# One step in thirteen of a graph attention gather, fetched row by row from SyncE and ScalarE

## The chip, the cores and the metric

The kernel runs on one core of a Trainium2 chip. The metric is the device time of one execution in microseconds (us), lower is better. Times below are medians of several executions; the profile is of one execution, recorded by the hardware profiler.

## The reference

One graph attention layer with a residual, over 12,500 nodes of 128 features and 412,500 edges of 64 features. The edges are sorted by target, and there are 4 heads of 32:

```python
h = maximum(layernorm(x), 0)
h = (h @ W_node.T).reshape(nodes, 4, 32)
e = (edge_attr @ W_edge.T).reshape(edges, 4, 32)
att = sum(concat([h[src], h[tgt], e], -1) * a, -1)
att = where(att > 0, att, 0.2 * att)
m = maximum(segment_max(att, tgt), 0)
ex = exp(att - m[tgt])
denom = segment_sum(ex, tgt) + (num_edges - deg)[:, None] * exp(-m)
out = x + segment_sum((ex / denom[tgt])[:, :, None] * h[src], tgt)
```

## The kernel before, in words

**Layout.** The sorted edges are padded and cut into 128 runs of T = 3224 edges, one run to a partition. One step is one edge of every partition, and a block is KB = 13 steps, so that there are 248 blocks. A node's row, 136 floats (544 bytes), lies in DRAM in `rows`: for each head 32 features and a one, then the four source logits.

**Setup.** The first stretch counts edges per node, projects the nodes, writes `rows` to DRAM, and builds the target logits `td`, which stay in SBUF for all edges.

**The block loop.** Eight blocks (UN) are unrolled; the first eight run outside the loop and the loop repeats them 30 times. For block i each engine has its own program, and engines meet in semaphores alone:

- GpSimd (`body`, L327) waits until the multiply of block i - 4 has read its slot group (`val_done`), then issues 13 indirect gathers (L334, by the helper at L291). Each fetches 128 rows, one to a partition, by one column of `idx`. There are SLOTS = 4 slot groups, so gathers may run up to four blocks ahead.
- VectorE first forms the logits of block i (`logits`, from L540; it waits for the gathers at L544), with small operations on 52 or 56 columns, and then the sums of block i - 1 (`sums`, from L568): a multiply of rows with weights (L571, signals `val_done`), a carry copy, and one scan (L581, signals `scanned`).
- ScalarE (`body`, L394) makes two exponentials (L399, L401) for block i, and copies the state of block i - 1 out of the scan's tile into `R` (`copy_state`, L412), which frees that tile and hands `R` to SyncE.
- SyncE (`body`, L261) stores `R` to DRAM (`store`, L257), loads the edge features of two blocks at once (L270), and every fourth block the node numbers of the next four (L266).
- TensorE multiplies the edge features with the edge weights, two blocks at once (L732).

Every engine takes its own instructions in the order in which they are written, and the DMAs that SyncE and GpSimd issue stand in those same orders. The addresses of DMAs in the loop hang on the loop's counter, so each is preceded by small register instructions on the issuing engine.

**Tail.** GpSimd fetches the last state of each node from DRAM, VectorE divides and adds x, and SyncE stores the output.

Of the kernel before, what the change touches and what calls it, by code (L numbers as in the profile page):

```python
# [4 lines left out]
P = 128  # L5
# [7 lines left out]
NP = P * W  # L13
T = 3224
KB = 13
BLOCKS = T // KB
PAIRS2 = BLOCKS // 2
SLOTS = 4
# [4 lines left out]
CL = 512  # L23
# [5 lines left out]
STEPS = W // NG  # L29
UN = 8  # L30
ITERS = BLOCKS // UN
RING = 8
PIECES = 8
PT = T // PIECES


def graph_attention_kernel(nc, x, x_t, src, dstf, dst16, lasts, ends, first, ea, w_node, w_node_t, a_blk, we2,
                           ident_c, centre_c, cols_c, out):
    fp32, bf16, i32, i16 = mybir.dt.float32, mybir.dt.bfloat16, mybir.dt.int32, mybir.dt.int16
    ALU = mybir.AluOpType  # L40
# [1 line left out]
    ds = bass.ds  # L42
# [8 lines left out]
    with ctx:  # L51
        def sb(name, shape, dt):
            return ctx.enter_context(nc.sbuf_tensor(name, shape, dt))
# [4 lines left out]
        def sem(name):  # L58
            return ctx.enter_context(nc.semaphore(name))
# [3 lines left out]
        hT = big[:, 0:NP]  # L63
        xr = big[:, 0:NP].rearrange("p (w d) -> p w d", d=D)
        idx = sb("idx", [P, 2, SLOTS * KB], i32)
        slots = sb("slots", [P, SLOTS * KB, ROW], fp32)
        V = sb("V", [P, 2, ROW * COL], fp32)
        R = sb("R", [P, 2, KB, ROW], fp32)
# [85 lines left out]
        idx_dma = [sem(f"idx_dma{k}") for k in range(2)]  # L154
        ea_dma = [sem(f"ea_dma{k}") for k in range(2)]
        gather_dma = [sem(f"gather_dma{k}") for k in range(SLOTS)]
        store_dma = [sem(f"store_dma{k}") for k in range(2)]
        ae_done, logits_done, d_ready, w_ready, a_ready, val_done, scanned, copied = (
            sem("ae_done"), sem("logits_done"), sem("d_ready"), sem("w_ready"), sem("a_ready"), sem("val_done"),
# [2 lines left out]
            sem("end_packed"), sem("end_t"), sem("mf_done"), sem("fac_done"), sem("sf_done"), sem("end_back"),  # L162
            sem("fix_gather"), sem("fix_max"), sem("fix_exp"), sem("fix_ready"), sem("fix_dma"))
        get_dma = [sem(f"get_dma{k}") for k in range(STEPS)]
        slots_taken = sem("slots_taken")
        em_done, group_done, stored = sem("em_done"), sem("group_done"), sem("stored")
        x_again = [sem(f"x_again{k}") for k in range(STEPS // 2)]

# [2 lines left out]
        def after(eng, s, v):  # L171
            if not (isinstance(v, int) and v <= 0):
                eng.wait_ge(s, v)  # L173

        def loop(eng, body):
            for q in range(UN):
# [44 lines left out]
        @block.sync  # L221
        def _(sp):
            sp.dma_start(last_b[:, :], lasts.broadcast_to([P, CL])).then_inc(loaded_lasts, 16)
            sp.dma_start(cols[:, :], cols_c).then_inc(loaded_lasts, 16)
            for a, b in ((w_raw, w_node), (we_raw, we2), (a_sb, a_blk), (centre, centre_c), (ident, ident_c)):
                sp.dma_start(a[:, :], b).then_inc(loaded_w, 16)
            sp.dma_start(w_ext[:, 0:D], w_node_t).then_inc(loaded_w, 16)
            for g in range(STEPS):
                sp.dma_start(hT[:, g * NG * P:(g + 1) * NG * P], x_t[:, g * NG * P:(g + 1) * NG * P]).then_inc(loaded_x[g], 16)
            sp.dma_start(dst_s, dstf).then_inc(loaded_dst, 16)  # L230
            sp.dma_start(ends_s[:, :], ends).then_inc(loaded_ends, 16)
            sp.dma_start(first_i[:, :], first).then_inc(loaded_ends, 16)
            sp.wait_ge(zeroed, 1)
            sp.dma_start(state_d[P * T:P * T + 1, :], zero_row[:, :]).then_inc(zero_stored, 16)
            sp.wait_ge(filled, 1)
            td_rows = tdst_d[0:P * T, :].rearrange("(p t) h -> p (t h)", p=P)
            for k in range(H):
                sp.dma_start(td_rows[:, k * T:(k + 1) * T], fill).then_inc(tdst_filled, 16)
            sp.dma_start(idx[:, 0, :], src[:, 0:SLOTS * KB]).then_inc(idx_dma[0], 16)
            for g in range(STEPS):  # L240
                sp.wait_ge(rows_ready, g + 1)
                sp.dma_start(rows.rearrange("(p w) r -> p w r", p=P)[:, g * NG:(g + 1) * NG, :], row_t[g % 2]).then_inc(rows_stored[g % 2], 16)
                if g == 6:
                    sp.wait_ge(tdst_filled, 64)
                    for d in range(2):
                        sp.dma_start(eab[:, d, :], ea[d * P:(d + 1) * P, :]).then_inc(ea_dma[d], 16)
            sp.dma_start(tnode_d.rearrange("(p w) h -> p (w h)", p=P), tnode[:, :, :].rearrange("p w h -> p (w h)")).then_inc(tnode_stored, 16)
            sp.wait_ge(rest_ready, 1)
            sp.dma_start(rest_d.rearrange("(p w) a -> p (w a)", p=P), rest[:, :]).then_inc(rest_stored, 16)
            sp.wait_ge(scattered, 16 * W)  # L250
            for k in range(PIECES):
                a, b = k * PT * H, (k + 1) * PT * H
                sp.dma_start(big[:, a:b], td_rows[:, a:b]).then_inc(td_dma[k], 16)

            state_rows = state_d[0:P * T, :].rearrange("(p t) r -> p (t r)", p=P)

            def store(b, k):  # L257
                sp.wait_ge(copied, b + 1)
                sp.dma_start(state_rows[:, ds(b * (KB * ROW), KB * ROW)], R[:, k, :, :].rearrange("p t r -> p (t r)")).then_inc(store_dma[k], 16)

            def body(it, q):  # L261
                i = it * UN + q
                if q % SLOTS == 0:
                    j = it * 2 + q // SLOTS
                    after(sp, gather_dma[SLOTS - 1], j * (16 * KB))
                    sp.dma_start(idx[:, 1 - q // SLOTS, :], src[:, ds(j * (SLOTS * KB) + SLOTS * KB, SLOTS * KB)]).then_inc(idx_dma[1 - q // SLOTS], 16)  # L266
                if q % 2 == 0:
                    d = it * (UN // 2) + q // 2
                    sp.wait_ge(ae_done, d + 1)
                    sp.dma_start(eab[:, q // 2 % 2, :], ea[ds(d * P + 2 * P, P), :]).then_inc(ea_dma[q // 2 % 2], 16)  # L270
                if not (isinstance(i, int) and i == 0):
                    store(i - 1, 1 - q % 2)

            loop(sp, body)
            store(EB - 1, 1)

            sp.wait_ge(d_ready, EB)
            for m in range(STEPS // 2):
                a, b = m * 2 * NG, (m + 1) * 2 * NG
                sp.dma_start(xr[:, a:b, :], x.rearrange("(p w) d -> p w d", p=P)[:, a:b, :]).then_inc(x_again[m], 16)  # L280
            o = out[0:NP, :].rearrange("(p w) d -> p w d", p=P)
            for g in range(STEPS):
                sp.wait_ge(group_done, g + 1)
                sp.dma_start(o[:, g * NG:(g + 1) * NG, :], xr[:, g * NG:(g + 1) * NG, :]).then_inc(stored, 16)
            sp.wait_ge(stored, 16 * STEPS)
            sp.wait_ge(fix_dma, 16)

        @block.gpsimd
        def _(pool):
# [37 lines left out]
            def body(it, q):  # L327
                s = q % SLOTS
                if s == 0:
                    pool.wait_ge(idx_dma[q // SLOTS], it * 16 + 16)  # L330
                after(pool, val_done, it * UN + q - SLOTS + 1)
                pool.sem_inc(slots_taken, 1)  # L332
                for j in range(KB):
                    gather(slots[:, s * KB + j, :], rows[:, :], idx[:, q // SLOTS, s * KB + j:s * KB + j + 1], gather_dma[s])  # L334

            loop(pool, body)
# [6 lines left out]
            for k in range(2):  # L343
                pool.wait_ge(store_dma[k], 16 * (BLOCKS // 2))
            pool.wait_ge(val_done, BLOCKS)
            gather(s_first[:, :], state_d[:, :], fe_i[:, 0:1], fix_gather)
            for g in range(STEPS):
                if g >= 7:
# [9 lines left out]
        def _(act):  # L358
# [35 lines left out]
            def body(it, q):  # L394
                i = it * UN + q
                v = q % 2
                act.wait_ge(d_ready, i + 1)
                after(act, val_done, i - 1)
                nc.scalar.activation(w_exp[v], D1[:, v, :], ACT.Exp).then_inc(w_ready, 1)  # L399
                after(act, scanned, i)  # L400
                nc.scalar.activation(a_all.rearrange("p (h v t) -> p h v t", h=H, v=HB),  # L401
                                     D2[:, v, :].rearrange("p (h a t) -> p h a t", h=H, a=1).broadcast_to([P, H, HB, COL]),
                                     ACT.Exp).then_inc(a_ready, 1)
                if not (isinstance(i, int) and i == 0):
                    copy_state(i - 1, 1 - v, it, q)

            def copy_state(b, k, it, q):
                if isinstance(b, int):
# [2 lines left out]
                    after(act, store_dma[k], it * (8 * UN) + 16 * ((q - 1) // 2))  # L411
                nc.scalar.copy(R[:, k, :, :], vcols(k)[:, :, 1:COL].rearrange("p c t -> p t c")).then_inc(copied, 1)  # L412

            loop(act, body)
            act.wait_ge(scanned, EB)
            copy_state(EB - 1, 1, 0, 0)
# [16 lines left out]
        def _(dve):  # L433
# [106 lines left out]
            def logits(it, q):  # L540
                i = it * UN + q
                v = q % 2
                s = q % SLOTS
                dve.wait_ge(gather_dma[s], it * (32 * KB) + 16 * KB * (q // SLOTS + 1))  # L544
                nc.vector.tensor_tensor(hk(z[:, :]), slots[:, s * KB:(s + 1) * KB, VAL:ROW].rearrange("p t h -> p h t"),  # L545
                                        td[:, ds(i * KB, KB), :].rearrange("p t h -> p h t"), ALU.add)
                dve.drain()
# [258 lines left out]
```

## Time and profile before

| | us |
|---|---|
| median of 3 runs | 4519.24 |
| lowest, highest | 4519.19, 4522.25 |
| the profiled execution's own time | 4519.71 |
| its span, first to last instruction | 4517.7 |

Busy shares of the span are in the first group of rows below. An engine's busy time leaves out register, branch, semaphore and DMA-issuing instructions, so SyncE has no busy time at all, and what it does is read from its queue (SPq in the rows). "issue" is idle time of an engine for which no wait is shown. The profile's 40 slices look alike from the third slice to the last but one: the block loop is nearly the whole of the run.

### The profile page before, as it was taken

Reading aid. Unit: us, or ns where it says so; the run is one execution under the profiler, and the core shown is the slowest. Engines: PE = TensorE matmul, PEld = TensorE weight load, DVE = VectorE, ACT = ScalarE, POOL = GpSimd, SP = SyncE. Lnnn points to the kernel's source line nnn. Section 1 sums busy time; section 2 is a strip of 40 time slices with the busy share of each in tenths; the row PEclk is TensorE's granted clock in tenths of the full one; section 3 lists DMA queues with packets and bytes.
Section 4 is the critical chain, followed back from the end, with each engine's and each line's share of the span. In section 5 each row is a group of like instructions: output and inputs, shape, how many; then the busy total and the mean of one; then the engine's idle time right before and its main releaser. Section 6 shows DMA issues by size and latency. Waiting matters only on the chain.

```text
span 4517.7 us, 21382 instructions
## 1 busy us (share of the span) xinstructions
PE 819.8 (18%) x3685; PEld 777.8 (17%) x3685; DVE 2492.8 (55%) x3230; ACT 1366.4 (30%) x1008; POOL 3382.6 (75%) x3532
## 2 busy tenths in 40 slices
PE   6301111112121211111121212121111112121200
PEld 4301111111111111111111111111111111111100
DVE  7516555555555555555555555555555555555553
ACT  8103333333333333333333333333333333333320
POOL 6777777777777777777777777777777777777756
PEclk6655555555555555555555555555555555555555
DMA  7424444444444444444444444444444444444453
GB/s 265 131 90 136 138 134 141 130 141 135 142 135 142 135 142 135 138 139 132 138 134 142 135 142 135 142 134 142 135 134 140 130 141 135 142 135 142 134 171 97
DMA packets 189542, 627.98 MB, mean 139 GB/s; under 512 B 74865, under 2 KB 75634, under 8 KB 188882
## 3 DMA queue, kind: packets, MB, share of 16 engines
q0 software_dynamic: 115936, 252.37, 23.3%
q1 hardware_dynamic: 73586, 375.40, 22.5%
q8 instruction: 5, 0.08, 0.0%
q14 instruction: 15, 0.12, 0.0%
HBM read 382.66 MB, written 244.86 MB: 139 GB/s over the span
## 4 chain that ended last, share of the span: by engine, by line
POOL 72%; issue 24%; DMA 1%; DVE 1%; PE 0%; POOLq 0%; ACT 0%; DVEq 0%; SPq 0%; ACTq 0%
POOL slots L291 70%; POOL tdst_scratch L294 1%; DMA V<-in_dst_dram,chunk_i 1%; POOL V L291 1%; DVE pen L448 1%; PE ae L721 0%; DVE slots L463 0%; POOL rstd L304 0%; POOLq L173 0%; DVE V L571 0%; ACT pen L364 0%; DMA rows_scratch<-slots 0%; DMA state_scratch<-R 0%; POOLq L332 0%; DVE V L581 0%
## 5 line engine op out<-in xcount | busy, mean ns | idle before, releaser
L291 POOL DMA_INDIRECT slots<-rows_scratch,idx x3224 | 3076.0, 954 | 982.4 <-issue 982.4
L732 PE MATMUL ae<-w_att,eab 128*128 128x8 f32 x3224 | 707.0, 361 | 3375.0 <-DVE z L550 3373.2
L732 PEld LDWEIGHTS ae<-w_att,eab 128*128 128x128 f32 x3224 | 696.3, 331 | 3385.8 <-DVE z L550 2433.3
L581 DVE TENSOR_TENSOR_SCAN V<-A,V 128x1848 f32<-128x1848 f32 x248 | 993.6, 4007 | 18.1
L401 ACT ACTIVATE A<-D 128x1848 f32<-128x1848 f32 x248 | 425.1, 1714 | 1849.3 <-DVE V L581 1849.3
L545 DVE TENSOR_TENSOR z<-slots,big 128x52 f32<-128x52 f32 x248 | 62.3, 251 | 1567.4 <-DMA slots<-rows_scratch,idx 1567.4
L412 ACT COPY R<-V 128x1768 f32<-128x1768 f32 x248 | 791.1, 3190 | 2.8 <-DVE V L581 2.8
L571 DVE TENSOR_TENSOR V<-slots,wexp 128x1716 f32<-128x1716 f32 x124 | 401.6, 3239 | 13.8
L571 DVE TENSOR_TENSOR V<-slots,extra 128x1716 f32<-128x1716 f32 x124 | 400.5, 3230 | 13.7
L399 ACT ACTIVATE wexp<-D 128x52 f32<-128x52 f32 x124 | 27.0, 218 | 562.5 <-DVEq L566 562.5
L399 ACT ACTIVATE extra<-D 128x52 f32<-128x52 f32 x124 | 27.0, 218 | 475.4 <-DVEq L566 475.4
L291 POOL DMA_INDIRECT V<-in_dst_dram,chunk_i x99 | 96.8, 977 | 45.3 <-issue 23.5
L448 DVE TENSOR_SCALAR_CACHE_REDUCE pen<-V,cols 128x806 bf16<-128x806 int16 x99 | 101.6, 1051 | 36.9 <-DMA V<-in_dst_dram,chunk_i 34.8
L294 POOL DMA_INDIRECT tdst_scratch<-tnode,put_i x98 | 94.8, 967 | 29.8 <-issue 29.4
L291 POOL DMA_INDIRECT slots<-state_scratch,get_i x98 | 93.2, 951 | 29.9 <-issue 29.9
L557 DVE TENSOR_TENSOR_SCAN V<-pen,att 128x56 f32<-128x56 f32 (+1 forms) x248 | 72.8, 294 | 47.9 <-issue 45.8
L564 DVE SCALAR_TENSOR_TENSOR D<-pen,dm 128x52 f32<-128x52 f32 (+1 forms) x248 | 52.9, 213 | 40.9 <-issue 40.3
L578 DVE COPY V<-V 128x132 f32<-128x132 f32 x247 | 75.0, 304 | 0.0
L364 ACT ACTIVATE pen<-last_b,half_n 128x512 bf16<-128x512 f32 x99 | 69.9, 713 | 0.0
L550 DVE TENSOR_TENSOR z<-z,ae 128x52 f32<-128x52 f32 x248 | 51.7, 208 | 27.6 <-issue 4.9
L554 DVE SCALAR_TENSOR_TENSOR att<-z 128x52 f32<-128x52 f32 x248 | 52.7, 213 | 22.9
L562 DVE COPY att<-V 128x4 f32<-128x4 f32 x248 | 64.8, 261 | 0.0
(148 smaller groups left out, 535.2 us busy)
## 6 DMA issues: line engine op xcount, KB each, us to landing
state_scratch<-R SPq DMA_DIRECT2D x248, 884.0 KB, 4.2
eab<-in_ea_dram SPq DMA_DIRECT2D x126, 832.0 KB, 6.3
slots<-rows_scratch,idx POOLq DMA_INDIRECT x3224, 2.6
rows_scratch<-slots SPq DMA_DIRECT2D x14, 476.0 KB, 2.5
tdst_scratch<-eab SPq DMA_DIRECT2D x4, 1612.0 KB, 30.9
big<-tdst_scratch SPq DMA_DIRECT2D x8, 806.0 KB, 10.9
big<-in_x_t_dram SPq DMA_DIRECT2D x14, 448.0 KB, 8.3
big<-in_x_dram SPq DMA_DIRECT2D x7, 896.0 KB, 11.8
```

Source lines behind the costliest of these rows:

```text
L291: pool.indirect_dma_start(buf, None, table, bass.IndirectOffsetOnAxis(ap=index, axis=0)).then_inc(done, 16)
L294: pool.indirect_dma_start(table, bass.IndirectOffsetOnAxis(ap=index, axis=0), buf, None).then_inc(done, 16)
L364: nc.scalar.activation(junk_a[k % 9], last_b[:, :], ACT.Sign, bias=half_n[:, k:k + 1], scale=-1.0, accum_out=sgn[:, k:k + 1])
L401: nc.scalar.activation(a_all.rearrange("p (h v t) -> p h v t", h=H, v=HB), D2[:, v, :].rearrange("p (h a t) -> p h a t", h=H, a=1).broadca ...
L412: nc.scalar.copy(R[:, k, :, :], vcols(k)[:, :, 1:COL].rearrange("p c t -> p t c")).then_inc(copied, 1)
L448: nc.vector.tensor_scalar(junk_v[k % RING], ring[:, k % RING, :], cols[:, k:k + 1], None, ALU.is_lt, ALU.add, accum_out=within[:, k:k + 1] ...
L557: nc.vector.tensor_tensor_scan(mcols(v), pen[:, ds(i, 1), :, :].rearrange("p a h t -> p (a h t)"), att[:, :], 0.0, ALU.min, ALU.max)
L562: nc.vector.tensor_copy(hk(att[:, :])[:, :, 0:1], hk(mcols(v))[:, :, KB:COL])
L571: nc.vector.tensor_tensor(v4[:, :, :, 1:COL], slots[:, s * KB:(s + 1) * KB, 0:VAL].rearrange("p t (h v) -> p h v t", h=H), w_exp[k].rearra ...
L578: nc.vector.tensor_copy(vcols(k)[:, 0:VAL, 0:1], vcols(1 - k)[:, 0:VAL, KB:COL])
L581: nc.vector.tensor_tensor_scan(V[:, k, 0:VAL * COL], a_all, V[:, k, 0:VAL * COL], 0.0, ALU.mult, ALU.add).then_inc(scanned, 1)
L732: last = mm(ps_ae[k][:, n * 2 * H:(n + 1) * 2 * H], eab[:, k, n * P:(n + 1) * P], w_att[:, :], start=True, stop=True)
```

## The change

Of the 13 gathers of a block GpSimd keeps 12 (KP = 12). The rows of the 13th step, 128 of them, are fetched by 128 DMAs of one row each: rows for partitions 0 to 63 are issued by SyncE (SPN = 64), those for partitions 64 to 127 by ScalarE (ACN = 64). The node numbers of these steps come in a new input `single`, by a new tile `sidx` on partition 0; each issuing engine loads 16 of them at a time from there into its registers and uses each as the address of one DMA. The rows of block i + 2 are issued in block i's body, after `val_done` of block i - 2, at the end of each engine's body. VectorE waits for both groups beside the gathers.

```diff
+KP = KB - 1
+SPN = 64
+ACN = P - SPN
+        sidx = sb("sidx", [1, 2, SLOTS * P], i32)
+        def single_rows(eng, q, p0, n, done):
+            half, base = q // SLOTS, q % SLOTS * P
+            for a in range(p0, p0 + n, 16):
+                _, at = nc.values_load_multi_w_load_instructions(
+                    sidx[0:1, half, base + a:base + a + 16], engines=(eng.engine,), min_val=0, max_val=NP - 1,
+                    skip_runtime_bounds_check_because="node numbers of the input")
+                for j in range(16):
+                    eng.dma_start(slots[a + j:a + j + 1, q % SLOTS * KB + KP, :], rows[ds(at[j], 1), :]).then_inc(done, 16)
...
 # SyncE, before its loop
+            for k in range(2):
+                sp.wait_ge(rows_stored[k], 16 * (STEPS // 2))
+                sp.wait_ge(sidx_dma[k], 16)
+            for q in range(2):
+                single_rows(sp, q, 0, SPN, row_dma_sp[q])
...
 # SyncE, body, at its end
                 if not (isinstance(i, int) and i == 0):
                     store(i - 1, 1 - q % 2)
+                ahead(it, q)
+
+            def ahead(it, q):
+                a = (q + 2) % UN
+                if a % SLOTS == 0:
+                    sp.wait_ge(sidx_dma[a // SLOTS], it * 16 + (16 if q + 2 < UN else 32))
+                after(sp, val_done, it * UN + q - 1)
+                sp.sem_inc(sp_rows, 1)
+                single_rows(sp, a, 0, SPN, row_dma_sp[a])
+                if a % SLOTS == SLOTS - 1:
+                    sp.wait_ge(sidx_taken, it * UN + q + 1)
+                    sp.dma_start(sidx[:, a // SLOTS, :],
+                                 single[:, ds((it * 2 + (q + 2) // SLOTS) * (SLOTS * P) + 2 * SLOTS * P, SLOTS * P)]).then_inc(sidx_dma[a // SLOTS], 16)
...
 # GpSimd, body
-                for j in range(KB):
+                for j in range(KP):
                     gather(slots[:, s * KB + j, :], rows[:, :], idx[:, q // SLOTS, s * KB + j:s * KB + j + 1], gather_dma[s])
...
 # ScalarE, body, after copy_state
+                a = (q + 2) % UN
+                if a % SLOTS == 0:
+                    act.wait_ge(sidx_dma[a // SLOTS], it * 16 + (16 if q + 2 < UN else 32))
+                    act.sem_inc(act_rows, 1)
+                after(act, val_done, i - 1)
+                act.sem_inc(act_rows, 1)
+                single_rows(act, a, SPN, ACN, row_dma_act[a])
+                act.sem_inc(sidx_taken, 1)
...
 # VectorE, logits
-                dve.wait_ge(gather_dma[s], it * (32 * KB) + 16 * KB * (q // SLOTS + 1))
+                dve.wait_ge(gather_dma[s], it * (32 * KP) + 16 * KP * (q // SLOTS + 1))
+                dve.sem_inc(block_begun, 1)
+                dve.wait_ge(row_dma_sp[q], it * (16 * SPN) + 16 * SPN)
+                dve.sem_inc(block_begun, 1)
+                dve.wait_ge(row_dma_act[q], it * (16 * ACN) + 16 * ACN)
```

ScalarE too issues the rows of blocks 0 and 1 before its loop.

## Rows read from the trace of the kernel before

**Rows 1.** The page, busy time by engine: us, share of the span, instructions.

```profile
PE 819.8 (18%) x3685; PEld 777.8 (17%) x3685; DVE 2492.8 (55%) x3230; ACT 1366.4 (30%) x1008; POOL 3382.6 (75%) x3532
```

**Rows 2.** The page, the chain that ended last: shares by engine, by line.

```profile
POOL 72%; issue 24%; DMA 1%; DVE 1%; PE 0%; POOLq 0%; ACT 0%; DVEq 0%; SPq 0%; ACTq 0%
POOL slots L291 70%; POOL tdst_scratch L294 1%; DMA V<-in_dst_dram,chunk_i 1%; POOL V L291 1%; DVE pen L448 1%; PE ae L721 0%; DVE slots L463 0%; POOL rstd L304 0%; POOLq L173 0%; DVE V L571 0%; ACT pen L364 0%; DMA rows_scratch<-slots 0%; DMA state_scratch<-R 0%; POOLq L332 0%; DVE V L581 0%
```

**Rows 3.** Instruction groups, 500 to 4300 us: busy us, mean ns | idle before, releaser.

```profile
L291 POOL DMA_INDIRECT slots<-rows_scratch,idx x3026 | 2878.9, 951 | 922.0 <-issue 922.0
L581 DVE TENSOR_TENSOR_SCAN V<-A,V 128x1848 f32<-128x1848 f32 x233 | 933.5, 4007 | 17.0
L412 ACT COPY R<-V 128x1768 f32<-128x1768 f32 x233 | 743.2, 3190 | 0.0
...
L401 ACT ACTIVATE A<-D 128x1848 f32<-128x1848 f32 x233 | 399.4, 1714 | 1722.9 <-DVE V L581 1722.9
L571 DVE TENSOR_TENSOR V<-slots,wexp 128x1716 f32<-128x1716 f32 x117 | 379.1, 3240 | 13.3
```

**Rows 4.** Waits, 500 to 4300 us: total us, times, longest.

```profile
DVE z L545 <- DMA slots<-rows_scratch,idx: 1473.1, 232, 6.7
POOL slots L291 <- issue: 922.0, 3026, 0.3
```

**Rows 5.** Timeline, mid loop: start us, duration us, engine, instruction.

```profile
2000.31 0.22 ACT L399 ACTIVATE extra<-D 128x52 f32<-128x52 f32 x1 [3.91 <-DVEq L566]
...
2012.74 0.95 POOL L291 DMA_INDIRECT slots<-rows_scratch,idx  x1 [0.30 <-issue]
...
2014.00 0.95 POOL L291 DMA_INDIRECT slots<-rows_scratch,idx  x1 [0.30 <-issue]
```

**Rows 6.** Timeline of SyncE's queue at the start of the run.

```profile
3.54 0.43 SPq L226 DMA_DIRECT2D ident<-in_ident_dram  x1
4.01 0.43 SPq L227 DMA_DIRECT2D w_ext<-in_w_node_t_dram  x1
...
12.99 0.44 SPq L232 DMA_DIRECT2D first_i<-in_first_dram  x1
13.47 1.32 SPq L234 DMA_DIRECT2D state_scratch<-zero_row  x1
...
21.22 1.86 SPq L239 DMA_DIRECT2D idx<-in_src_dram  x1
```

**Rows 7.** Timeline of SyncE's queue over eight blocks of the loop.

```profile
446.44 0.36 SPq L266 DMA_DIRECT2D idx<-in_src_dram  x1
...
478.60 0.35 SPq L270 DMA_DIRECT2D eab<-in_ea_dram  x1
...
577.12 0.35 SPq L266 DMA_DIRECT2D idx<-in_src_dram  x1
```

**Rows 8.** SyncE's instructions of L259, L270 and L242: ns min/median/max, first and last start.

```profile
L259 SPq DMA_DIRECT2D state_scratch<-R x248: 332/343/361, 343.2 to 4370.1; - x124
L259 SPq FUSED_REGOPS  x240: 37/43/57, 461.5 to 4364.1; - x120
L259 SPq MOVE state_scratch<-R x240: 29/29/29, 461.6 to 4364.2; - x120
...
L270 SPq FUSED_REGOPS  x120: 55/60/66, 446.9 to 4332.1; - x120
...
L242 SPq DMA_DIRECT2D rows_scratch<-slots x14: 319/320/327, 157.0 to 210.1; - x14
```

**Rows 9.** DMA issues: count, KB each, median us from issue to landing.

```profile
centre<-in_centre_dram SPq DMA_DIRECT2D x1, 64.0 KB, 2.1
ident<-in_ident_dram SPq DMA_DIRECT2D x1, 64.0 KB, 1.9
```

**Rows 10.** DMA queues: packets, MB, share of 16 engines' span.

```profile
q0 software_dynamic: 115936, 252.37, 23.3%
q1 hardware_dynamic: 73586, 375.40, 22.5%
```

**Rows 11.** Windows, the loop: us; busy us (count) by engine; clock, DMA share, GB/s.

```profile
430.00:4367.00 3937.00, 679.33 (x3094) 668.94 (x3094) 2214.02 (x2655) 1220.11 (x725) 2969.33 (x3121) 0.50 0.46 137
```

More of the change, by code:

```diff
@@ L32, with graph_attention_kernel @@
 RING = 8
+KP = KB - 1
+SPN = 64
+ACN = P - SPN
 PIECES = 8
 PT = T // PIECES
-def graph_attention_kernel(nc, x, x_t, src, dstf, dst16, lasts, ends, first, ea, w_node, w_node_t, a_blk, we2,
+def graph_attention_kernel(nc, x, x_t, src, dstf, dst16, lasts, ends, first, single, ea, w_node, w_node_t, a_blk, we2,
                            ident_c, centre_c, cols_c, out):
@@ L156, in graph_attention_kernel @@
         gather_dma = [sem(f"gather_dma{k}") for k in range(SLOTS)]
+        sidx_dma = [sem(f"sidx_dma{k}") for k in range(2)]
+        row_dma_sp = [sem(f"row_dma_sp{k}") for k in range(UN)]
+        row_dma_act = [sem(f"row_dma_act{k}") for k in range(UN)]
+        sidx_taken = sem("sidx_taken")
         store_dma = [sem(f"store_dma{k}") for k in range(2)]
@@ L164, in graph_attention_kernel @@
         get_dma = [sem(f"get_dma{k}") for k in range(STEPS)]
-        slots_taken = sem("slots_taken")
+        slots_taken, block_begun, act_rows, sp_rows = sem("slots_taken"), sem("block_begun"), sem("act_rows"), sem("sp_rows")
         em_done, group_done, stored = sem("em_done"), sem("group_done"), sem("stored")
@@ L239, in _ @@
             sp.dma_start(idx[:, 0, :], src[:, 0:SLOTS * KB]).then_inc(idx_dma[0], 16)
+            for k in range(2):
+                sp.dma_start(sidx[:, k, :], single[:, k * SLOTS * P:(k + 1) * SLOTS * P]).then_inc(sidx_dma[k], 16)
             for g in range(STEPS):
@@ L253, in _ @@
                 sp.dma_start(big[:, a:b], td_rows[:, a:b]).then_inc(td_dma[k], 16)
+            for k in range(2):
+                sp.wait_ge(rows_stored[k], 16 * (STEPS // 2))
+                sp.wait_ge(sidx_dma[k], 16)
+            for q in range(2):
+                single_rows(sp, q, 0, SPN, row_dma_sp[q])
             state_rows = state_d[0:P * T, :].rearrange("(p t) r -> p (t r)", p=P)
@@ L264, in body @@
                     j = it * 2 + q // SLOTS
-                    after(sp, gather_dma[SLOTS - 1], j * (16 * KB))
+                    after(sp, gather_dma[SLOTS - 1], j * (16 * KP))
                     sp.dma_start(idx[:, 1 - q // SLOTS, :], src[:, ds(j * (SLOTS * KB) + SLOTS * KB, SLOTS * KB)]).then_inc(idx_dma[1 - q // SLOTS], 16)
@@ L272, in body @@
                     store(i - 1, 1 - q % 2)
+                ahead(it, q)
[10 more added lines that the diff above has]
+                                 single[:, ds((it * 2 + (q + 2) // SLOTS) * (SLOTS * P) + 2 * SLOTS * P, SLOTS * P)]).then_inc(sidx_dma[a // SLOTS], 16)
             loop(sp, body)
             store(EB - 1, 1)
+            for k in range(2):
+                sp.wait_ge(sidx_dma[k], (ITERS + 1) * 16)
             sp.wait_ge(d_ready, EB)
@@ L345, in _ @@
             pool.wait_ge(val_done, BLOCKS)
+            for a in range(2):
+                pool.wait_ge(row_dma_sp[a], (ITERS + 1) * 16 * SPN)
+                pool.wait_ge(row_dma_act[a], (ITERS + 1) * 16 * ACN)
             gather(s_first[:, :], state_d[:, :], fe_i[:, 0:1], fix_gather)
@@ L412, in copy_state @@
                 nc.scalar.copy(R[:, k, :, :], vcols(k)[:, :, 1:COL].rearrange("p c t -> p t c")).then_inc(copied, 1)
+            for k in range(2):
+                act.wait_ge(rows_stored[k], 16 * (STEPS // 2))
+                act.wait_ge(sidx_dma[k], 16)
+            for q in range(2):
+                single_rows(act, q, SPN, ACN, row_dma_act[q])
             loop(act, body)
@@ L777 @@
     ends[:-1, 3] = dst2[1:, 0]
+    single = _np.zeros((1, (BLOCKS + 3 * SLOTS) * P), _np.int32)
+    single[0, :BLOCKS * P] = srcp.reshape(P, BLOCKS, KB)[:, :, KB - 1].T.reshape(-1)
     eap = _np.zeros((P * T, K), f4)
@@ L791 @@
         "x": xp, "x_t": xt, "src": _np.concatenate([srcp.reshape(P, T), _np.zeros((P, SLOTS * KB), _np.int32)], axis=1), "dstf": dst2.astype(f4), "dst16": dst512.astype(_np.int16),
-        "lasts": dst512[:, -1].astype(f4).reshape(1, CL), "ends": ends, "first": dst2[:, 0:1], "ea": eat,
+        "lasts": dst512[:, -1].astype(f4).reshape(1, CL), "ends": ends, "first": dst2[:, 0:1], "single": single, "ea": eat,
         "w_node": w_node, "w_node_t": w_node.T, "a_blk": a_blk, "we2": _np.concatenate([w_edge, w_edge], axis=1),
```

## The prediction

> **What bounds the kernel now.** I read the page from the top. The busy times come first: GpSimd is busy 75% of the span, VectorE 55%, ScalarE 30% [rows 1]. Busy shares don't say who waits for whom, so the chain of waits is next: 70% of it is GpSimd's gathers into `slots`, and 24% is "issue" [rows 2]. The groups of the loop's middle say what that issue time is: each gather takes 951 ns, and the idle time before the gathers is 922.0 us over 3026 of them, 0.305 us each, with no other engine behind it [rows 3, 4]. The timeline agrees: two gathers start 1.26 us apart [rows 5]. So GpSimd goes from gather to gather without a pause, and 13 x (0.951 + 0.305) = 16.33 us is its block. SyncE's node-number loads stand two groups of four apart at 446.44 and 577.12 us: 130.68 / 8 = 16.34 us per block [rows 7]. The two agree, so nothing else sets the pace.
>
> VectorE has slack: it waits 1473.1 us for gathers, 232 times, which is 6.35 us of each block, and so needs 16.34 - 6.35 = 9.99 us [rows 4]. ScalarE's block is 0.22 + 1.71 + 3.19 = 5.12 us [rows 3, 5]. SyncE issues one store per block at 0.343 us, half an edge load at 0.35 us and a quarter of a number load at 0.36 us, together 0.6 us [rows 7, 8].
>
> **The change, part by part.**
>
> *GpSimd.* One gather of 13 goes: 12 x 1.256 = 15.07 us, 1.26 us less. Over 248 blocks that is worth 248 x 1.256 = 311 us, if nothing else takes longer than 15.07 us for a block. That is the whole possible gain.
>
> *What stands in its place.* SyncE and ScalarE each issue 64 DMAs for every block, in series with everything else in their programs. All three, GpSimd, SyncE and ScalarE, now have to finish their share before VectorE can start a block, so the slowest of them sets the pace. I therefore price one issue.
>
> 1. The DMA instruction. The trace has SyncE's issues in two settings. One that follows a pause takes 0.320 us (L242) to 0.343 us (L259) [rows 8]. Those issued back to back at the start take 0.43 us and start 0.47 us apart: 3.54, 4.01 [rows 6]. The duration hardly hangs on size: `first_i`, 512 bytes in all, takes 0.44 us, as much as a matrix of 64 KB. Sixty-four in a row are back to back, so I take 0.43 us, and 0.47 us from start to start.
> 2. The address. Each loop DMA is preceded by a fused register operation (43 ns at L259, 60 ns at L270) and a move (29 ns) [rows 8]. Some of that may lie in the pause of 0.04 us between two issues. I take 0.03 us beyond it: 0.50 us per row. The ends are 0.320 + 0.029 = 0.35 us and 0.44 + 0.04 + 0.060 + 0.029 = 0.57 us.
> 3. So 64 x 0.50 = 32.0 us per engine and block (22.4 to 36.5 us).
> 4. Loading 64 node numbers from SBUF into registers. No row shows such a load. From below it costs at least what a move costs, 29 ns per register, 1.9 us per block. From above I take the small ScalarE instruction that reads and writes SBUF, 0.22 us [rows 5], per register: 14 us. The nearest row is a register operation at 60 ns, so 4 us.
> 5. The rest of the program. SyncE has its 0.6 us and a quarter of a number load for `sidx`. ScalarE has 5.12 us of exponentials and copies; these run in its datapath, and whether its queue goes on issuing DMAs meanwhile no row shows, since ScalarE issues no DMA now. It costs between 0 and 5.1 us. I take 2 us, since the first two instructions release the waits of VectorE while the copy alone (3.19 us) stands right before the DMAs.
>
> The sum is 32.0 + 4 + 2 = 38 us per block against 16.34 us, and the ends are 22.4 + 1.9 + 0.6 = 24.9 and 36.5 + 14 + 5.1 = 55.6 us. ScalarE is the slower of the two issuers, and SyncE goes in step with it, because its store of block i - 1 waits for ScalarE's copy.
>
> *Who is behind the issuing engines.* On ScalarE the exponentials of block i + 1 are queued behind the 64 issues of block i's body, and VectorE's multiply waits for them. It is no longer hidden, but it costs no further time: VectorE's 9.99 us lie beside 38 us of issues. The two blocks of lead do not help against a rate, only against a delay.
>
> *The total.* The issues of all blocks form one row of work from the end of the setup. `td` is fetched at 289 us, after which SyncE starts its first loop loads at 293 us; it then issues 250 sets (two ahead, two beyond the end, whose last stands in front of the tail's loads), and what follows takes about the 165 us that now lie between the last gather's landing and the end of the span. T = 293 + 250C + 165 = 458 + 250C. With C = 16.34 this gives 4543, 0.5% above the profiled execution (4519.7, itself 0.5 us from the median of the runs), so it is good enough here. With C = 38: 458 + 9500 = 9958, say 9960 us. The ends: C = 24.9 gives 6680, C = 55.6 gives 14,360.
>
> *Two pages against the rows.* The start-to-start time of 0.47 us for small DMAs [rows 6] is the number on which all this hangs. The Trainium skill says in DMA: Bandwidth & Descriptors, section "Issuing engines are not separate DMA queues", that issuing from several engines saves only the sequencer's time to initiate a DMA, "which is usually small relative to the DMA itself". By that rule the issues would be small and the kernel would come near the gain on GpSimd; the rows speak against it, since one issue takes 0.43 us here. The same page, section "Latency and other measured facts", gives a floor of about 600 ns for a register load from memory; no run here shows one. With one load for 16 numbers it would be 2.4 us per block, estimated from that page, and with one load for each number 38 us.
>
> **The rivals.**
>
> *A. A single-row issue is much cheaper and GpSimd still sets the pace: faster.* All rows of the trace move 128 partitions except one, `zero_row`, and if the 0.43 us are spent on 128 rows, one row may cost a fraction. The point from which it decides: SyncE and ScalarE must both stay under 15.07 us, so (15.07 - 0.7) / 64 = 0.22 us per row with its address and its number. Then T = 4519.7 - 311 = 4208 us. For it: nothing shows that one row costs what 128 cost. Against it: the only single-row issue took 1.32 us [rows 6], though a queue that was full may have held it up, for the 26 KB number load took 1.86 us shortly after and takes 0.36 us in the loop [rows 7]; and register work alone is 0.07 us.
>
> *B. Cheaper, but still the bound.* At 0.25 to 0.35 us per row, all in, C is 17 to 23 us, and T with 20 us is 5460 us. It rests on the same argument as A with less of it.
>
> *C. The DMA engines set the pace.* The 115,936 packets of GpSimd's queue took 23.3% of 16 engines' span [rows 10]: 0.233 x 16 x 4517.7 / 115,936 = 0.145 us each. If each row makes a data packet and a semaphore packet, and all fall on the same engines, that is 128 x 2 x 0.145 = 37 us per block, and with the 0.46 x 16.3 = 7.5 us that each is busy now [rows 11], 44.6 us. T = 458 + 250 x 44.6 = 11,600 us. Against it: small packets should take less than the mean of packets that are mostly larger. Landing does not hold issues back at this pace: at the start a DMA issued every 0.47 us landed after 1.9 to 2.1 us without growing later [rows 6, 9].
>
> *D. SyncE and ScalarE can't issue at the same time.* If both need one piece of hardware for the 0.47 us, the block costs 128 x 0.47 + 4 = 64 us, and T = 16,500 us. No row has two engines issuing direct DMAs, so nothing speaks for or against.
>
> **How the numbers follow.** Forecast 0.66; A 0.06; B 0.12; C 0.08; D 0.07; the last 0.01 for no change at all. The forecast is 9960 us. The range has to reach past the forecast's own ends, on the low side to take in part of B's neighbourhood and on the high side C and the dear loads: 6700 to 14,400 us leaves out A, most of B and D, which together are about 0.2. Faster by over 0.2%, about what a measurement of this kernel tells from no change, is A: 0.06. Within 0.2%: 0.01. Slower: 0.93.
>
> **What would show it.** In the changed kernel's profile, GpSimd's gathers still take 0.951 us but wait for VectorE's multiply; GpSimd's busy share falls to about 3170 / 9960 = 32%. VectorE waits some 28 us per block, for rows. SyncE's queue is a solid row of DMAs about 0.5 us apart with 0.43 us each. If that duration is under 0.2 us for one row, steps 1 and 3 are wrong and A or B holds. If it is 0.9 us or more on both engines while they overlap, D holds. If the time from issue to landing grows far beyond 2 us and issues lengthen with it, C holds. If the space between issues is far over 0.1 us, or there are pauses of some us before each 16, step 4 is wrong. The prediction as a whole fails if the block's period comes out under 16.34 us.

## The result, and the profile after

The changed kernel takes 9365.44 us (median of 4 runs, 9356.04 to 9375.52) against 4519.22 us: a ratio of 2.0721, with a 95% interval of 2.0685 to 2.0757. The forecast was 9960 us in a range of 6700 to 14,400 us. It is slower for the reason forecast, that the issuing engines set the pace, and the time is about 6% under the forecast; but the engine that sets it is SyncE and not ScalarE.

The head of the page after, the answer to [rows 1 and 2], then the DMA queues, the answer to [rows 10]:

```profile
span 9358.0 us, 120779 instructions
...
PE 826.4 (9%) x3685; PEld 782.9 (8%) x3685; DVE 2455.3 (26%) x3230; ACT 1366.5 (15%) x1008; POOL 3139.5 (34%) x3284
...
q1 hardware_dynamic: 105714, 384.30, 12.5%
q0 software_dynamic: 108000, 235.09, 10.0%
q10 hardware_dynamic: 32000, 8.77, 0.5%
q14 instruction: 942, 7.72, 0.3%
...
SPq 72%; issue 25%; POOL 3%; DMA 1%; DVE 0%; ACT 0%; POOLq 0%; DVEq 0%; ACTq 0%
SPq L190 50%; SPq L186 19%; SPq L283 1%; POOL tdst_scratch L333 1%; POOL slots L330 1%; SPq L294 1%; POOL V L330 0%; DMA V<-in_dst_dram,chunk_i 0%; DVE pen L503 0%; SPq L290 0%; SPq L308 0%; POOL rstd L343 0%; SPq L282 0%; ACT pen L406 0%; SPq L304 0%
```

The busy times of VectorE and ScalarE are those of before within 2%, in twice the span, and GpSimd's is 7% less, for it issues 248 gathers fewer: no computation has become dearer. The chain has passed from GpSimd to SyncE's queue, which has no busy time on the page at all. Half of the chain is SyncE's row DMAs with the register operations and moves that stand on the same line (L190; 16,000 x (0.225 + 0.037 + 0.029) = 4656 us of 9358), 19% are its register loads (L186), and the 25% "issue" are mostly the pauses between these instructions.

The waits between 500 and 9100 us, over 240 blocks (the answer to [rows 4]):

```profile
DVE z L604 <- DMA slots<-rows_scratch: 6209.5, 240, 30.3
POOL slots L330 <- DVE V L630: 5026.8, 240, 25.3
```

VectorE waits 25.9 us in each block for rows, where it waited 6.35 us for gathers. GpSimd now waits 20.9 us per block for a slot to come free. What happens between two stores of SyncE (its queue alone; start us, duration us):

```profile
5028.82 0.63 SPq L190 DMA_DIRECT2D slots<-rows_scratch  x2
5029.70 0.39 SPq L283 DMA_DIRECT2D state_scratch<-R  x1
5033.09 30.32 SPq L190 DMA_DIRECT2D slots<-rows_scratch  x64
5063.70 0.36 SPq L290 DMA_DIRECT2D idx<-in_src_dram  x1
5064.36 0.35 SPq L294 DMA_DIRECT2D eab<-in_ea_dram  x1
5064.96 0.36 SPq L283 DMA_DIRECT2D state_scratch<-R  x1
5069.54 0.29 SPq L190 DMA_DIRECT2D slots<-rows_scratch  x1
```

The queue has no wait in the loop, for ScalarE's copy neither; these two stores stand 35.26 us apart. Between a store and the first row of the next set there are 3.0 us in one block and 4.2 us in the other, and the instructions of the two lines say what fills them. For all rows and loads (ns min/median/max, first and last start), and then for the load behind the store at 5029.70, the three later ones of that set, and the one behind the store at 5064.96:

```profile
L190 ACTq DMA_DIRECT2D slots<-rows_scratch x16000: 213/213/1001, 221.0 to 9182.0; - x198
L190 SPq FUSED_REGOPS  x16000: 37/37/46, 294.1 to 9209.4; - x198
L190 SPq MOVE slots<-rows_scratch x16000: 29/29/37, 294.2 to 9209.5; - x198
L190 SPq DMA_DIRECT2D slots<-rows_scratch x16000: 224/225/381, 294.3 to 9209.6; - x198
...
L186 SPq TENSOR_LOAD <-sidx x1000: 1171/1239/4320, 292.9 to 9201.7; - x167
...
L186 SPq TENSOR_LOAD <-sidx x1: 2707/2707/2707, 5030.2 to 5030.2; - x1
...
L186 SPq TENSOR_LOAD <-sidx x3: 1227/1229/1238, 5039.6 to 5055.6; - x3
...
L186 SPq TENSOR_LOAD <-sidx x1: 3929/3929/3929, 5065.4 to 5065.4; - x1
```

A row costs SyncE 0.225 us for the DMA, and two rows that stand together take 0.63 us, so 0.63 - 0.225 = 0.41 us from one to the next: 0.037 + 0.029 us of register work and 0.12 us of pauses around it. Sixty-four rows are 26.2 us. One load fetches 16 numbers. Three of a set's four take 1.24 us, the first takes 2.7 or 3.9 us, so loads are 3 x 1.24 + 3.3 = 7.0 us. A block takes (9209.6 - 294.3) / 250 = 35.66 us on average, so the rest of it is 2.4 us. Some of the rest is a pause of 2.8 us before a number load, seen at 5205.6 and at 5491.5, once in eight blocks, for which the trace shows no wait; its cause is open.

### The profile page after: what moved, and what is told of

Its sections match the earlier page's. It is cut to its first block, busy times and chain, and to the rows that moved or that the text cites. A ratio compares the mean times of both kernels' runs of the same rounds, so it can differ in the third digit from the quotient of the medians.

```text
span 9358.0 us, 120779 instructions
## 1 busy us (share of the span) xinstructions
PE 826.4 (9%) x3685; PEld 782.9 (8%) x3685; DVE 2455.3 (26%) x3230; ACT 1366.5 (15%) x1008; POOL 3139.5 (34%) x3284
## 4 chain that ended last, share of the span: by engine, by line
SPq 72%; issue 25%; POOL 3%; DMA 1%; DVE 0%; ACT 0%; POOLq 0%; DVEq 0%; ACTq 0%
SPq L190 50%; SPq L186 19%; SPq L283 1%; POOL tdst_scratch L333 1%; POOL slots L330 1%; SPq L294 1%; POOL V L330 0%; DMA V<-in_dst_dram,chunk_i 0%; DVE pen L503 0%; SPq L290 0%; SPq L308 0%; POOL rstd L343 0%; SPq L282 0%; ACT pen L406 0%; SPq L304 0%
## 5 line engine op out<-in xcount | busy, mean ns | idle before, releaser
L330 POOL DMA_INDIRECT slots<-rows_scratch,idx x2976 | 2832.6, 952 | 5935.4 <-DVE V L630 5101.5
L609 DVE TENSOR_TENSOR z<-z,ae 128x52 f32<-128x52 f32 x248 | 51.7, 208 | 27.6 <-issue 4.9
L619 DVE TENSOR_TENSOR D<-att,V 128x52 f32<-128x52 f32 x248 | 53.1, 214 | 18.8 <-issue 0.4
```

The lines of the kernel that those rows point to most:

```text
L330: pool.indirect_dma_start(buf, None, table, bass.IndirectOffsetOnAxis(ap=index, axis=0)).then_inc(done, 16)
```

## The experiments

All are the changed kernel with one edit, unless said otherwise; the fences show the lines that matter, and the waits and counters that go with them are changed too. Runs 1 to 6 leave rows out or fetch the wrong ones. Run 1 was timed twice, runs 7, 9 and 12 four or five times, all others once.

**1. Nothing in place of the 13th gather** (on the kernel before).

```diff
-                for j in range(KB):
+                for j in range(KB - 1):
                     gather(slots[:, s * KB + j, :], ...
```

> Twelve gathers per block and nothing in place of the 13th (its rows are left out, so the time is that of less work). Theory 1 (the gather that goes is worth its full pitch when nothing else is slower): 248 x 1.256 = 311 us less, 4208 us. Rival (another engine holds the block near 16 us, so the gather was hidden): 4400 us or more.

Measured: 4213.55 us (2 runs), ratio 0.9314 (0.927 to 0.9359). The kernel before took 4519.82 us beside it. A gather is worth its pitch: 306 us against 311 expected. That is all there is to gain.

**2 and 3. One issuing engine alone.**

```diff
 # 2: SyncE alone, the ScalarE rows left out
-                single_rows(act, a, SPN, ACN, row_dma_act[a])
 # 3: ScalarE alone, the SyncE rows left out
-                single_rows(sp, a, 0, SPN, row_dma_sp[a])
```

> Only SyncE's 64 rows of the 13th step are fetched, ScalarE's 64 are left out. Theory 1 (SyncE's own program sets the pace: 64 rows x 0.42 us, 7.0 us of register loads, 1.8 us of the rest, about 35.7 us a block): time unchanged, 9300 to 9400 us, row DMAs stay at 0.225 us. Rival 2 (the two issuing engines get in each other's way): the row DMAs get shorter than 0.2 us and the time falls below 8500 us.

> Only ScalarE's 64 rows are fetched, SyncE's 64 are left out. Theory 1: ScalarE alone needs 64 x 0.386 + 4 x 1.3 = 30 us for its rows and about 1 us more that is not under them, so 31 us a block and about 8200 us. Rival 2 (the queues get in each other's way): 7500 us or less. Rival 3 (ScalarE's exponentials and copy are added in full, 5.1 us): 35 us a block, 9200 us.

Measured: 9367.96 us with SyncE alone, where both together take 9365; 8382.19 us with ScalarE alone. SyncE's row DMAs in run 2, to be laid beside those of the changed kernel:

```profile
L190 SPq DMA_DIRECT2D slots<-rows_scratch x16000: 224/225/306, 295.5 to 9217.3; - x198
```

Taking ScalarE's 16,000 DMAs away changes neither the time nor the 225 ns. So SyncE's program alone is the pace, and the two queues do not take turns. ScalarE alone comes to (8380 - 458) / 250 = 31.7 us a block, so its 5.1 us of exponentials and copies are not added to its roughly 30 us of rows. The timeline of the changed kernel shows it directly (ScalarE and its queue):

```profile
5005.06 0.49 ACTq L190 DMA_DIRECT2D slots<-rows_scratch  x1
5005.17 3.19 ACT L462 COPY R<-V 128x1768 f32<-128x1768 f32 x1
5005.70 29.23 ACTq L190 DMA_DIRECT2D slots<-rows_scratch  x63
5035.18 0.22 ACT L441 ACTIVATE wexp<-D 128x52 f32<-128x52 f32 x1 [26.82 <-issue]
```

Row DMAs start at 5005.06 and 5005.70 while the copy runs from 5005.17 to 5008.36. Only what is written behind the rows waits: the next exponential comes at 5035.18.

**4 and 5. Fixed addresses**, without register loads and register operations; in 5 SyncE alone.

```diff
-                _, at = nc.values_load_multi_w_load_instructions(...)
-                    eng.dma_start(slots[...], rows[ds(at[j], 1), :]).then_inc(done, 16)
+                    eng.dma_start(slots[...], rows[97 * (a + j):97 * (a + j) + 1, :]).then_inc(done, 16)
```

> All 128 row DMAs are issued, but from fixed addresses (always the same 128 rows, so the data are not the edges'), without register loads, register operations and moves. Theory 1: 64 x (0.225 + 0.05) = 17.6 us and 1.8 us of the rest on SyncE, 19.4 us a block, about 5300 us. Rival 4 (a row DMA cannot follow another faster than every 0.41 us, whatever stands between them): 64 x 0.41 + 1.8 = 28 us, about 7460 us.

> As the run with fixed addresses, but ScalarE's rows are left out too, so SyncE issues 64 row DMAs a block, from fixed addresses, alone. With both engines issuing, both went at 0.295 us from start to start in undisturbed stretches and were held up beside the gathers. Theory 2 (both engines draw on one thing, which gives each a DMA every 0.295 us): alone the pitch falls to 0.213 + 0.042 = 0.255 us, and the time to 458 + 250 x 18.5 = 5100 us. Rival 5 (the floor is each queue's own): the pitch stays 0.295 us and the time near 7350 us.

Measured: 7354.48 us for 4, 5841.92 us for 5. The row DMAs of run 4 in a stretch of 6 us in which none is drawn out, then those of run 5 in such a stretch and right behind a store and an edge load:

```profile
L187 ACTq DMA_DIRECT2D slots<-rows_scratch x21: 265/266/283, 3999.9 to 4005.8; - x21
L187 SPq DMA_DIRECT2D slots<-rows_scratch x21: 252/253/266, 4000.1 to 4006.0; - x21
```

```profile
L187 SPq DMA_DIRECT2D slots<-rows_scratch x38: 252/252/268, 2999.9 to 3010.8; - x38
...
L187 SPq DMA_DIRECT2D slots<-rows_scratch x12: 256/294/452, 3013.1 to 3017.2; - x12
```

In the even stretches the pace is the same with one issuer or two: (3010.8 - 2999.9) / 37 = 0.295 us alone, (4006.0 - 4000.1) / 20 = 0.295 us together. So the two engines do not draw on one thing for it, and theory 2's reason for 5100 us falls. But rival 5's time of 7350 us for run 5 was missed too: the pitch stayed and the time fell. And neither 5300 nor 7460 us was right for the reasons given for run 4: with fixed addresses a row is 0.295 us and not 0.275 or 0.41, and that 7460 us lies near 7354 is luck. In run 5, (5840 - 458) / 250 = 21.5 us, of which 64 x 0.295 = 18.9 us are rows at this pace. The gathers do not hold the rows up: in run 5's even stretch GpSimd issued nine of them. The longer DMAs behind it, from 3013.1 us, follow an edge load at 3012.04 and a store at 3012.66, with no gather started between 3011.96 and 3018.72.

In run 4 the block is 27.6 us, 6 us more than with SyncE alone. The chains of the two pages show what changed (run 4's by line, then the landing of a store in run 4 and in run 5):

```profile
DMA slots<-rows_scratch 31%; SPq L187 31%; DVE V L637 7%; DVE V L627 5%; ACT R L459 5%; ACTq L187 3%; POOL slots L327 1%; POOL tdst_scratch L330 1%; SPq L280 1%; POOL V L327 1%; DMA V<-in_dst_dram,chunk_i 1%; DVE V L613 0%; DVE z L601 0%; D
...
state_scratch<-R SPq DMA_DIRECT2D x248, 884.0 KB, 12.1
```

```profile
state_scratch<-R SPq DMA_DIRECT2D x248, 884.0 KB, 4.0
```

With both engines issuing every 0.295 us or so, transfers land late: a row issued at 3012.17 us landed 18.73 us later by the chain, a store takes 12.1 us in place of 4.0, and 31% of the chain is the landing of rows, which has 0% in run 5 and in the changed kernel. VectorE starts late for it, ScalarE's copy follows VectorE, and SyncE waited for that copy, 958.1 us in 157 waits, which run 2's never did. The row DMAs get longer as well, with medians of 257 ns (SyncE) and 284 ns (ScalarE) over the whole run. So at this faster pace rival C's sign appears, and the landing is the largest new item. What makes the rows land late (their number, or that it is always the same 128 rows) these runs do not separate.

**6. Half of the rows**: 32 per engine.

> Half of the rows: SyncE and ScalarE fetch 32 each, with addresses and register loads as in the change; the other 64 rows of the 13th step are left out. Theory 1: SyncE's block is 32 x 0.42 + one load of 3.2 us + one of 1.24 us + 1.8 us = 19.7 us, 5380 us. Rival (a fixed cost per block, a wait for landing, dominates): above 7000 us.

Measured: 5311.10 us, 1.3% from the expectation. The sum per row, per load and per block scales as it should; no fixed wait shows behind it.

**7. SyncE's rows ahead of its store.**

```diff
-                if not (isinstance(i, int) and i == 0):
-                    store(i - 1, 1 - q % 2)
                 ahead(it, q)
+                if not (isinstance(i, int) and i == 0):
+                    store(i - 1, 1 - q % 2)
```

> SyncE issues the rows of block i + 2 before the store of block i - 1, so that the first register load of a set no longer stands behind a store of 884 KB. Theory 6 (a register load waits behind the large DMA just issued on its queue: 2.7 to 3.9 us against 1.24 us): the first loads fall to 1.24 us, 2.1 us a block less, 8850 us. Rival 7 (the first load of a set is slow for another reason, or ScalarE, with its 37 us between two sets, takes over): within 1% of 9360 us.

Measured: 9174.95 us, ratio to the kernel before 2.0304 (2.027 to 2.0338), so 190 us less than the change, 0.76 us per block and not 2.1. The direction is theory 6's, but I had overlooked that in every other block nothing stands between the last store and the rows any more, so that the first load still follows a store:

```profile
L186 SPq TENSOR_LOAD <-sidx x1000: 1135/1233/2680, 293.1 to 9007.0; - x167
```

The maximum falls from 4.3 to 2.68 us. Between 5000 and 5300 us the first loads of the blocks without an edge load still take 2.5 to 2.7 us, and the others take 1.1 to 1.9 us, where in the changed kernel they took 3.8 to 4.2 us.

**8 and 10. Two probes behind the last DMA of the kernel before**: SyncE issues 8 DMAs in a row, 544 bytes on each of n partitions, and register loads in different company.

```diff
+            for n in (1, 2, 8, 16, 64, 128):      # 10: (32, 64, 96)
+                for j in range(8):
+                    sp.dma_start(slots[0:n, c, :], rows[8 * j:8 * j + n, :]).then_inc(probe, 16)
```

> The kernel before, and behind its last DMA SyncE issues groups of 8 back-to-back DMAs of 544 B per partition on 1, 2, 8, 16, 64 and 128 partitions, then register loads of 1, 4 and 16 values, then such loads right behind a row DMA, right behind a store of 884 KB, and after such a store has landed. Theory 8 (the issue costs by the number of DMA engines it spreads over): 0.22 us on 1 partition, 0.43 us from 16 partitions on, the same on 128. Rival 9 (it costs by rows): near 0.22 us still on 16, 0.43 us only on 128. Register loads: 1.24 us whatever the count if they are a round trip, 16 times the cost of one otherwise. Behind the store 2.7 us, after its landing 1.24 us.

> The kernel before, and behind its last DMA SyncE issues 8 back-to-back DMAs each on 32, 64 and 96 partitions, then register loads of 1, 4 and 16 values (each followed by one DMA that uses the last of them), three right behind a one-row DMA, three right behind a store of 884 KB, three after that store has landed. In the first probe 16 partitions took 0.420 us, 64 took 0.597, 128 took 0.432. If the cost follows the run of partitions per DMA engine, 32 and 96 lie between 0.42 and 0.8 us and 64 again at 0.597. Theory 6 (a load is a round trip that stands behind what its queue has just given to the DMA engines): 1.24 us for 1, 4 and 16 values alike, 1.24 us behind a one-row DMA, 2.7 us behind the store, 1.24 us after its landing. Rival (each value costs its own share): 16 values take several times what one takes.

Measured, in the order of the text: 1, 2, 8, 16, 64 and 128 partitions in probe 8, then 32, 64 and 96 in probe 10:

```profile
L290 SPq DMA_DIRECT2D slots<-rows_scratch x8: 247/252/254, 4510.5 to 4512.6; - x8
...
L290 SPq DMA_DIRECT2D slots<-rows_scratch x8: 223/253/255, 4513.8 to 4515.9; - x8
...
L290 SPq DMA_DIRECT2D slots<-rows_scratch x8: 263/296/298, 4517.3 to 4519.6; - x8
...
L290 SPq DMA_DIRECT2D slots<-rows_scratch x8: 308/420/422, 4521.2 to 4524.3; - x8
...
L290 SPq DMA_DIRECT2D slots<-rows_scratch x8: 525/596/597, 4525.9 to 4530.3; - x8
...
L290 SPq DMA_DIRECT2D slots<-rows_scratch x8: 347/432/435, 4532.5 to 4535.8; - x8
```

```profile
L290 SPq DMA_DIRECT2D slots<-rows_scratch x8: 348/421/423, 4510.8 to 4514.0; - x8
...
L290 SPq DMA_DIRECT2D slots<-rows_scratch x8: 571/596/597, 4515.6 to 4520.1; - x8
...
L290 SPq DMA_DIRECT2D slots<-rows_scratch x8: 321/426/428, 4522.4 to 4525.6; - x8
```

A back-to-back issue costs 0.25 us on 1 or 2 partitions, 0.30 on 8, and 0.42 to 0.43 on 16, 32, 96 and 128: it grows up to 16 and then stays, as theory 8 has it. Rival 9, a cost by rows, falls. The exception is 64 partitions with 0.60 us, in both probes, for which I have no shown cause. So the 0.43 us that the prediction read from 128-partition DMAs was the price of another kind of DMA.

Probe 8's trace has no register loads (nothing used their values), so it says nothing on them. Probe 10 has them: of 1 value, of 4, of 16, then 16 values behind a row DMA, behind the store, and after its landing:

```profile
L297 SPq TENSOR_LOAD <-idx x1: 479/479/479, 4527.5 to 4527.5; - x1
...
L297 SPq TENSOR_LOAD <-idx x1: 485/485/485, 4529.3 to 4529.3; - x1
...
L297 SPq TENSOR_LOAD <-idx x1: 1137/1137/1137, 4531.2 to 4531.2; - x1
...
L297 SPq TENSOR_LOAD <-idx x3: 1132/1222/1224, 4540.4 to 4546.0; - x3
...
L297 SPq TENSOR_LOAD <-idx x3: 2493/2497/2497, 4549.1 to 4557.6; - x3
...
L297 SPq TENSOR_LOAD <-idx x3: 1133/1134/1137, 4565.0 to 4577.1; - x3
```

One value costs as much as four, and 16 cost 1.14 us: neither a single round trip nor 16 shares, but as much as four steps of (1.14 - 0.48) / 3 = 0.22 us on a base of 0.26 us would (an estimate from these two numbers, and other splits fit them as well). Behind a store that has not landed the load takes 2.50 us, after the landing 1.13 us. Together with run 7 that shows the first loads of a set in the changed kernel to be late because of the store in front of them. Why the delay is 2.7 us in one block and 3.9 us in the other, with the edge load ahead of the store, was not tested by itself.

**11. 48 rows on SyncE, 80 on ScalarE** (SPN = 48).

> The change with SyncE fetching 48 rows and ScalarE 80. Theory 1 (each engine's own rows): SyncE 48 x 0.42 + 3.3 + 2 x 1.24 + 1.8 = 27.7 us, ScalarE 80 x 0.386 + 5 x 1.3 + 1.4 = 38.8 us, so ScalarE sets the pace, about 10,100 us. Rival 2 (only the sum of 128 rows counts): unchanged, 9360 us.

Measured: 10,302.07 us, that is (10,300 - 458) / 250 = 39.4 us a block against 38.8 expected (2% above the expected time). SyncE now waits for ScalarE's copy, 2599.8 us in 247 waits. The sum of the rows is the same and the time isn't, so it is the fuller engine that counts.

**9 and 12. Versions meant to gain**, on the kernel before: only one block in four has its last step fetched row by row, spread over three blocks.

```diff
+SP_ROWS = ((0, 28), (28, 56), (56, 72))        # 12: ((0, 32), (32, 64), (64, 80))
+ACT_ROWS = ((72, 92), (92, 112), (112, 128))   # 12: ((80, 96), (96, 112), (112, 128))
 # ScalarE, 9: between its first and its second exponential; 12: behind copy_state
+                if part < 3:
+                    single_rows(act, h, ACT_ROWS[part], row_dma_act[h])
```

> A version that is meant to gain: only one block in four has its 13th step fetched by rows, and its 128 rows are spread over three blocks (SyncE 28, 28 and 16 rows ahead of its store; ScalarE 20, 20 and 16 behind the first exponential, where it waits for the scan anyway). GpSimd issues 51 gathers in four blocks in place of 52. Theory 1 (an issuing engine's rows cost nothing as long as its own block stays under GpSimd's): SyncE needs 28 x 0.42 + 2 x 1.24 + 1.8 = 16 us in its fullest block and 11.9 us on average, so 4519.9 - 62 x 1.256 = 4442 us. Rival (rows arrive after the gathers, or ScalarE's late exponentials hold up VectorE, in the block that needs them): 4520 us or more.

> As the spread version (one block in four, 128 rows over three blocks), but ScalarE issues its rows behind its copy instead of ahead of its second exponential, 16 in each of the three blocks, and SyncE 32, 32 and 16. In the spread version VectorE waited 1259 us for ScalarE's copy, 199 times, and the second exponential waited behind row issues for 1630 us. Theory 10 (those rows delayed the copy of the block, for which VectorE's next block waits, and that ate the gain): the waits for the copy vanish and the time falls below before, 4442 to 4490 us. Rival (what is lost is SyncE's late rows, or the sheer number of issues): 4520 us or more.

Measured: 4609.50 us for 9 against 4531.33 us of the kernel before beside it, ratio 1.0173 (1.016 to 1.0187), and 4726.60 us for 12 against 4519.84 us, ratio 1.0457 (1.0442 to 1.0472). So 9 is 1.7% slower, a small difference but clear of its interval, 12 is 4.6% slower, and theory 1 and theory 10 missed; both times are in the range of their rivals. Waits of 9 and of 12, 500 to 4300 us:

```profile
DVE V L609 <- ACT R L456: 1259.4, 199, 10.2
```

```profile
DVE z L597 <- DMA slots<-rows_scratch: 966.1, 56, 18.9
...
DVE V L609 <- ACT R L456: 703.1, 166, 4.3
```

In 9 ScalarE's copy comes late, and VectorE needs it: the scan that the second exponential needs ended at 2014.58, but 20 rows stand ahead of it, from 2009.54 to 2018.14, so it starts at 2018.19, and its copy ends at 2023.03, for which VectorE had waited 7.79 us. In 12 the wait for the copy falls by nearly half, in theory 10's direction, but it does not vanish: 703.1 / 166 = 4.2 us of each remain. And in every fourth block VectorE now waits 966.1 / 56 = 17.3 us for rows, where in 9 it waited 340.9 / 57 = 6.0 us. SyncE's rows come last:

```profile
2018.46 0.23 SPq L189 DMA_DIRECT2D slots<-rows_scratch  x1
...
2020.23 0.25 DVE L597 TENSOR_TENSOR z<-slots,big 128x52 f32<-128x52 f32 x1 [18.47 <-DMA slots<-rows_scratch]
```

The last row of the set is issued at 2018.46, and VectorE starts 1.8 us later. A slot group is free only in the three blocks ahead of its use, and 80 rows with their loads do not fit beside SyncE's stores in that time. In the next set the group came free at 2039.56, when a multiply ended, and VectorE was ready for it at 2071.51, 32 us later; SyncE's rows ran from 2041.04 to 2085.05, 44 us. My average (11.9 us per block) hid both deadlines. No version beat the kernel before.

## Why the prediction was right, and where its sizes were off

*What bounded the kernel before*: GpSimd's gathers, and nothing else near. Shown by run 1, where one gather less gave its pitch.

*Step 1, the DMA instruction (0.43 us)*: nearly twice too dear. It is 0.225 us on SyncE and 0.213 us on ScalarE. I took the price of DMAs on 128 partitions; the probes show that it grows up to 16 partitions. Rival A's argument, that one row costs less than 128, was sound, but it needed 0.22 us for everything. The sign for A or B, under 0.2 us, was just missed.

*Step 2, the address (0.03 us)*: too cheap. I let the register work lie in the shadow of a pause between two DMAs. From DMA to DMA there are 0.41 - 0.225 = 0.185 us, where I had 0.07 us, and run 5 without addresses has 0.295 us from start to start, so the address adds about 0.11 us to the pitch. The two errors work against each other, -0.205 and +0.115 us, and leave a pitch of 0.41 us against 0.50.

*Step 3*: 26.2 us against 32.0, inside its ends (22.4 to 36.5).

*Step 4, the register loads (4 us)*: 7.0 us, inside 1.9 to 14. Four loads of 1.24 us would have been 5.0; the first of a set stands behind a store. This is what the sign for step 4 named: the space between issues is over 0.1 us, and there are pauses of 1.24 us and more before each 16. The Trainium skill's floor of about 600 ns (DMA: Bandwidth & Descriptors, "Latency and other measured facts") does not hold for this read from SBUF: one value took 0.44 and 0.48 us in probe 10.

*Step 5, the rest (2 us)*: 2.4 us, but of SyncE and not of ScalarE. ScalarE's compute lies mostly under its issues, and its row DMA takes 0.213 us, so SyncE is the slower issuer: 35.7 us a block against 31.7 us of ScalarE alone. "ScalarE is the slower of the two" was wrong, and runs 2 and 3 show it; nor does SyncE go in step with it, for SyncE never waits for its copy.

*The sum*: 35.7 us against 38. The formula 458 + 250C gives 9373 us for it, where the span is 9358. The mechanism was right, but that the time came within 6% is partly luck: 5.8 us too many for the rows stand against 3.0 us too few for the loads.

*The rivals.* A and B: the issue was indeed about half the price, but with register work and loads a row is (26.2 + 7.0) / 64 = 0.52 us, far above 0.22 and above B's 0.35. C: the 32,000 packets of ScalarE's rows took 0.5% of 16 engines' span, 0.005 x 16 x 9358 / 32,000 = 0.023 us each and not 0.145, so 128 rows are 6 us, and VectorE starts 1.6 us after the last row of a set is issued (5029.2 to 5030.80). At run 4's faster pace a packet took 0.018 x 16 x 7353 / 32,000 = 0.066 us and rows landed late, so C names a limit that comes next and not the one of this kernel. D: run 2 refutes it at this pace, and the even stretches of runs 4 and 5 at a faster one.

*VectorE's 9.99 us.* This played no part in the result, but it is too low as a floor. Taking its waits for gathers away lets another wait appear: in run 12 three of its blocks start 13.8 us apart (2029.95, 2043.75, 2057.59), with 4.2 to 4.3 us of waiting for ScalarE's copy in each.

## What to carry to other kernels

An indirect gather of 128 rows costs its engine 1.26 us, or 0.01 us per row; a register-addressed DMA of one row costs 0.5 us, fifty times that, and dividing such DMAs over two idle queues did not make up for it. Price such a row as the pitch of its whole sequence (register load, register operations, DMA) and compare the engine's full set with the period of the block, for each engine by itself. Before spreading work over queues that look idle, check what is written behind it and by when it must have landed: averages over blocks hid both in the two versions meant to gain.

## What the runs showed of the hardware that was not expected

- A back-to-back DMA issue took 0.596 us on 64 partitions and 0.42 to 0.43 us on 32, 96 and 128, in two probes. Open why.
- A register load of 16 values from SBUF took 1.14 us, of 1 or 4 values 0.44 to 0.49 us, and 2.50 us directly behind a store of 884 KB.
- Row DMAs with register work between them took 0.213 to 0.225 us each, but back to back they took 0.252 us and came every 0.295 us.
- With two engines issuing rows from fixed addresses (run 4), one row landed 18.7 us after its issue and a store of 884 KB took 12.1 us to land; with one (run 5) the store took 4.0 us.
